# Cross attention over a long context: mixes in bursts of six chunks instead of four, with the SBUF room laid out anew

## The reference

```python
def _L1_xattn_ref(query, key, value, Wq, bq, Wk, bk, Wv, bv, Wo, bo):
    Q = _proj(query, Wq, bq)          # (x @ W + b) as 16 heads of 32
    K = _proj(key, Wk, bk)
    V = _proj(value, Wv, bv)
    scores = jnp.einsum('bihd,bjhd->bijh', Q, K) * SCALE
    attn = jax.nn.softmax(scores, axis=1)
    x = jnp.einsum('bijh,bjhd->bihd', attn, V).reshape(B, S, D_MODEL)
    return x @ Wo + bo
...
x = x + _L1_xattn_ref(_layernorm(x, axis=-1), ctx_1024, ctx_1024, ...)
```

## Time and profile before

| what | value |
|---|---|
| median of 3 runs | 2689.61 us (2688.83 to 2691.11) |
| the profiled execution's own time | 2689.59 us |
| its span in the profile | 2687.9 us, 59612 instructions |
| mean granted TensorE clock | 0.991 of full speed |

### The profile page before, as it was taken

How to read it: one execution, slowest core, us unless ns; L and a number is a source line. 1 busy time by engine, 2 the same in 40 slices (tenths; PEclk the granted TensorE clock), 3 DMA queues, 4 the chain that set the end, 5 groups by cost and what they waited for, 6 DMA issues and landing times.

```text
span 2687.9 us, 59612 instructions
## 1 busy us (share of the span) xinstructions
PE 2612.9 (97%) x21096; PEld 2204.9 (82%) x21096; DVE 1967.7 (73%) x3889; ACT 1860.6 (69%) x6826; POOL 1267.2 (47%) x2200
## 2 busy tenths in 40 slices
PE   7998999999999999999999999999999998999998
PEld 5775899878888888888888888888888885799997
DVE  6876766577777778777777777777777776655555
ACT  2112444288888888888888888888888886355553
POOL 4432111155556556555655655565555552222222
PEclk9999999999999999999999999999999998999999
DMA  9994445456666666666666666666666653455551
GB/s 340 391 333 184 166 177 191 125 140 172 167 165 157 162 164 161 158 168 166 158 161 165 158 162 168 164 160 162 166 158 161 168 131 125 170 185 188 188 188 71
DMA packets 132300, 473.33 MB, mean 176 GB/s; under 512 B 31129, under 2 KB 31257, under 8 KB 124833
## 3 DMA queue, kind: packets, MB, share of 16 engines
q1 hardware_dynamic: 131616, 468.47, 61.0%
q10 hardware_dynamic: 384, 1.05, 0.2%
HBM read 244.47 MB, written 17.30 MB: 97 GB/s over the span
## 4 chain that ended last, share of the span: by engine, by line
PE 84%; SPq 5%; DVE 3%; DMA 3%; issue 2%; POOL 2%; ACT 1%; ACTq 0%; POOLq 0%; DVEq 0%
PE PB L584 18%; PE PB L609 13%; PE PB L597 11%; PE PB L617 11%; PE PB L685 7%; PE PB L700 6%; PE PB L414 6%; PE PB L546 6%; SPq L332 5%; PE PB L559 3%; DMA STK<-KHL 1%; PE PB L442 1%; PE PB L473 1%; POOL KHL L1484 1%; DMA AR<-in_ctx 1%
## 5 line engine op out<-in xcount | busy, mean ns | idle before, releaser
L825 ACT ACTIVATE EE<-PB,small 128x256 f32<-128x256 f32 x3136 | 1442.6, 481 | 213.6 <-DVE small L1207 199.8
L1207 DVE TENSOR_REDUCE small<-PB 128x2 f32<-128x512 f32 x1568 | 1029.9, 680 | 364.7 <-PE PB L609 364.4
L825 ACT ACTIVATION_READ_ACCUMULATOR EE<-PB,small 128x1 f32 x3136 | 664.3, 212 | 0.0
L1469 POOL TENSOR_TENSOR VS<-V,small 128x128 f32<-128x128 f32 x784 | 319.1, 407 | 710.5 <-DVE small L1213 702.6
L584 PE MATMUL PB<-CTX,WKV 128*128 128x256 f32 x4704 | 625.0, 282 | 3.1 <-POOL CTX L1457 3.1
L584 PEld LDWEIGHTS PB<-CTX,WKV 128*128 128x128 f32 x4704 | 588.4, 190 | 3.4 <-POOL CTX L1457 3.3
L609 PEld LDWEIGHTS PB<-QS,STK 128*128 128x128 f32 x3136 | 469.2, 190 | 127.6 <-issue 60.1
L609 PE MATMUL PB<-QS,STK 128*128 128x256 f32 x3136 | 555.2, 289 | 9.8 <-ACT EE L825 5.0
L597 PE MATMUL PB<-WKV,CTX 128*128 128x512 f32 x1584 | 433.6, 396 | 3.4 <-DVE V L1203 3.4
L617 PE MATMUL PB<-EE,VS 128*32 128x256 f32 x6272 | 382.7, 385 | 0.0
L597 PEld LDWEIGHTS PB<-WKV,CTX 128*128 128x128 f32 x1584 | 273.8, 191 | 40.2 <-DVE V L1203 4.2
(11 more groups left out here) (201 smaller groups left out, 2542.4 us busy)
## 6 DMA issues: line engine op xcount, KB each, us to landing
STK<-KHL SPq DMA_DIRECT2D x1568, 128.0 KB, 2.3
RW<-in_l1f SPq DMA_DIRECT2D x32, 2048.0 KB, 8.1
AR<-in_ctx SPq DMA_DIRECT2D x49, 1024.0 KB, 8.4
RAW<-in_ctx SPq DMA_DIRECT2D x98, 512.0 KB, 3.5
WF<-in_l0f SPq DMA_DIRECT2D x17, 2304.0 KB, 8.8
v_scr<-RAW SPq DMA_DIRECT2D x64, 256.0 KB, 8.2
V<-v_scr SPq DMA_DIRECT2D x64, 256.0 KB, 2.9
WA<-in_l0a SPq DMA_DIRECT2D x1, 4096.0 KB, 12.8
```

The costliest lines, as they stand in the source:

```text
L825: m = e.activation(EE[:, b, s, :], bank(2 * (k % 2) + half, 256 * (s % 2), 256), ACT.Exp, bias=nm[:, b, s:s + 1], accum_out=su[:, b, s:s + 1])
L1207: e.tensor_reduce(nm[:, k % RING, 2 * half:2 * half + 2], bank(2 * (k % 2) + half).rearrange("p (s i) -> p s i", s=2), axis=AX.X, op=ALU.m ...
L1469: e.tensor_tensor(VS[:, b, :].rearrange("p (s d) -> p s d", s=4), V[:, t % 4, 128 * c:128 * c + 128].rearrange("p (s d) -> p s d", s=4), r ...
```

## The change

Mixes come in bursts of six: the burst behind chunk k with k % 6 == 5 has the mixes of chunks k - 7 to k - 2. `EE`, `VS` and the small tiles of maxima, sums and reciprocals have eight places instead of six. 784 is four more than a multiple of six, so the loop leaves the last six mixes, 778 to 783, to a loop behind it. `OT` and `WO` now share room with the second half of `KHL` and the front of `STK`; `QHL` shares room with places 4 and 5 of `EE`. The load of `WO` moves on SP's queue from chunk 40 to behind the loop, and waits for the scores of chunk 775, the last to read the half of `STK` where `WO` is put.

```diff
-MIX = 4
-RING = 6
+MIX = 6
+RING = 8
...
         CTX = sb("CTX", [P, 3, 2, NC, GT], F32R, life)
+        late = ExitStack()
+        sb("khl_front", [P, 3, NC, GT], over=late)
+        OT = sb("OT", [P, NC, 256], over=late)
+        WO = sb("WO", [P, NC, D], over=late)
+        late.close()
         KHL = sb("KHL", [P, 2, 2, NC, GT], F32R, life)
...
         VS = sb("VS", [P, RING, P], over=life)
-        EE = sb("EE", [P, RING, 4, 256], over=life)
-        OT = sb("OT", [P, NC, 256], over=life)
         q_life = ExitStack()
+        sb("ee_front", [P, 4, 4, 256], over=q_life)
         QHL = sb("QHL", [P, 2, NC, 256], F32R, q_life)
         q_life.close()
-        WO = sb("WO", [P, NC, D], over=life)
+        EE = sb("EE", [P, RING, 4, 256], over=life)
...
-                if k == 40:
-                    w.wait_ge("d_q", 256)
-                    e.dma_start(WO[:, :, :], a["l1x"][:, 2048:4096].rearrange("p (c n) -> p c n", c=NC)).then_inc(S["d_wo"], 16)
...
+            w.wait_ge("s_mm", 2 * (NCH - 8))
+            e.dma_start(WO[:, :, :], a["l1x"][:, 2048:4096].rearrange("p (c n) -> p c n", c=NC)).then_inc(S["d_wo"], 16)
             w.wait_ge("vp_mm", v_count(NT - 1))
             e.dma_start(WL, a["l1a"]).then_inc(S["d_wl"], 16)
...
                 if k % MIX == MIX - 1:
                     for n in range(max(k - MIX - 1, 0), k - 1):
                         mix(n)
-            mix(NCH - 2)
-            mix(NCH - 1)
+            for n in range(NCH - NCH % MIX - 2, NCH):
+                mix(n)
```

## The result

The change makes the kernel slower by 94 us: 2784.1 us (2783.6 to 2784.6, four runs) against 2689.9 us, a ratio of 1.0355 with a 95% interval of 1.0341 to 1.0368. The direction was forecast; 2730 us and the range up to 2757 were not enough.

A forecast was written before the change was run, and what follows sets the result against it. TensorE, busy 97% of the span, was taken as the bound. Saved tile changes, ScalarE's waits and stacked K gave 53.4 against 52.2 us per 24 chunks, +39 us over 32 rounds, taken as +40: 2730 us, range 2703 to 2757.

The forecast's parts named there:

- Tile changes: At TensorE's mix bursts: 65 fewer bursts at 0.3 us per tile change and back, 20 us saved.
- a forecast of the whole change: TensorE stays the only bound, so the saved tile changes count whole: 2670 us; a rival with chance 0.13.
- ScalarE's waits: At the fifth chunk's scores in each run between bursts: 0.31 us waiting for exps, at least 1.24 us per 24 chunks.
- Stacked K: At group starts, scores wait for 16 `stack_k` transfers: short groups take 16.85 us instead of 16.50.
- short group: Group of eight chunks holding one burst of six, two of every three groups: 16.19 us by TensorE alone, 16.85 forecast.
- 15.9 to 17.3: Microseconds from a group boundary until the next-but-one group's stacked keys are there: 4.20 + 10.0 to 11.3 + 1.7.
- the places of the bursts: Bursts behind chunks 5, 11, 17 and 23 of 24, weighed for stacked K: 53.4 us per 24 chunks against 52.2.
- No cost for eight places, the layout and `WO`: Eight buffer places, buffers in other room and the later `WO` load at the end: each 0.
- VectorE "under its bound": In the chunk loop, VectorE is busy 1253 of 1590 us and stays under its bound.
- the clock's part: Granted clock lost in new waits would cost like slower transfers (2756 us, rival at 0.08); no wait exceeds 1 us.

The follow-up runs named there:

- Both edits: Changed kernel with GpSimd's low part of the context moved ahead in each chunk and 8 instead of 16 stacked K transfers per group: 2710.9 us.
- bursts of six and short exps: Changed kernel with context first on GpSimd, half the stacked K transfers, and exps over 128 of 256 queries from the ninth chunk on: 2672.6 us.
- all transfers: Changed kernel with only GpSimd's low part of the context moved ahead of scaled V and low K, all 16 stacked K transfers kept: 2739.1 us.
- the late context put back: Changed kernel with GpSimd's order unchanged and 8 instead of 16 stacked K transfers per group from the third group on: 2782.1 us.

## Why the prediction was wrong, step by step

- **Tile changes: right.** 65 x 0.3 us; four burst lengths give 0.31 to 0.33 each. The Trainium skill's rule in "TensorEngine Tiling (Array Packing)", Key Properties, that a change of mode drains the array, agrees with a price that doesn't depend on the burst's length, though no run shows that it is a drain; as a forecast of the whole change it would have had the sign wrong.
- **ScalarE's waits: right, at the upper end.** 0.31 us in each run and up to 0.3 more, 1.24 to 1.54 us per 24 chunks, were forecast. Both edits together leave 52.9 - 51.5 = 1.4 us. Net of the saved tile changes that is +20 us, measured.
- **Stacked K: right.** Forecast 16.85 us for a short group where the other waits give 16.50, so 0.7 us per 24 chunks; measured, with the context out of the way, 53.7 - 52.9 = 0.8 us, 28 us in all. The three groups of a round then take 17.0, 17.1 and 19.8 us in the mean, forecast were 16.85, 16.85 and 19.74. (The upper end of its "15.9 to 17.3" is 17.2 by its own terms; nothing hangs on it.)
- **The step that failed** is the one on the places of the bursts. It asked which transfer a group start waits for, and stopped at the scores. The same chunk's K projection waits too, for `ctx_lo` (the first wait in `project_k`), and it was costed at nothing without its cover being named. The cover was the burst behind chunk 7, with 0.56 us to spare. Measured: 55.1 - 53.7 = 1.4 us per 24 chunks, 45 us; the second and third groups of a round take 18.0 and 20.4 us instead of 16.85 and 19.74. GpSimd, with its 945 of 1590 us, was weighed as part of the stacked K's chain alone; but its work is in a fixed order behind waits, and the earlier trace rows themselves had GpSimd's low half of K coming 4 us after a group start.
- **No cost for eight places, the layout and `WO`: right**, within 3 us.
- **VectorE "under its bound"** was right of its sum, not of its order: with bursts of six and short exps some 13 us of waits are left, and the rows beside one of them have VectorE late.

The ladder in medians, from 2690.7: +20 to both edits (2710.9), +28 with all transfers (2739.1), +45 with the context last (2784.1). The forecast had the first two, +20 and +20 or so. The sizes of the last two hold for this order alone: with the late context put back ahead of the transfers it is +71 and then +2.

No kernel that computes the reference beat the one before. Its bursts of four behind chunks 3 and 7 are a good place: they cover GpSimd's context, give the transfers their time, and let ScalarE catch up before it is reached.

## What to carry to other kernels

When a block of work is moved in an engine's order, list every wait of the instructions that now come earlier, not only of the one that looks critical, and read for each by how much it is met today. A block that an engine runs without waiting is also the cover for all the others; its length against the smallest spare time behind it says what moving it uncovers. And an engine at half load can be the releaser that is late, if its work is queued behind a wait: look at the order before its share.

## What was not expected of the hardware

The price of a change of tiles and back is the same 0.31 to 0.33 us for 16, 32, 48 and 64 narrow matmuls, and TensorE's granted clock stayed at 1.00 in the loop through 54 us of waits for transfers, 54 for ScalarE (pauses behind bursts among both) and 45 at the K projection, none over 1.6 us. The prediction had put the clock's part at nothing because no wait would be longer than 1 us; the waits were longer, and the clock held all the same.
